# Adaptive-norm transformer layer on one core: the projection stage laid out in even slots, and the residual rows formed in the output stage

## The chip, the cores and the metric

One core of one Trainium2 chip runs the whole kernel as one program. The metric is the device time of one execution in microseconds (us). The engines are TensorE (PE in the profile, PEld for its weight loads), VectorE (DVE), ScalarE (ACT), GpSimd (POOL) and SyncE (SP), which issues the DMAs here.

## What is computed

The reference is one layer over x of shape 16 x 1024 x 256 (batches, rows, features), cut here to what the change touches:

```
sa, ca, ga, ... = six vectors of 256 per batch, from silu(c) @ wmod
h  = layernorm(x) * (1 + ca) + sa
xn = layernorm(h) * ln_gamma + ln_beta
q, k, v = xn @ Wq + bq, xn @ Wk + bk, xn @ Wv + bv      # 16 heads of 16
q, k = rope(q), rope(k)
out = softmax(mask(q k^T / 4)) v                         # causal, 1024 x 1024 per head
x  = x + ga * (h + out @ Wo + bo)
# then layernorm(x) * (1 + cb) + sb and a routed feed-forward part over the first two batches' rows
```

All is float32 to the output. The term `x + ga * h` of each row is called its residual row below. Written with the first norm `n = layernorm(x)`, it is `x + n * (ga * (1 + ca)) + ga * sa`; the factor `ga * (1 + ca)` is the row `M_A2` of the table of modulation rows (`mods_d`), and the constant part is in the output bias.

## The kernel before

The program has five stages, one after the other, each in a block of its own: `phase0` (tables and modulation rows), `phase1` (norms, projections, rope), `phase2` (attention), `phase3` (output projection and residual) and `phase4` (feed-forward). The change is in `phase1` and `phase3`. A batch is T = 8 tiles of 128 rows by 256 features.

**The projection stage** (`phase1`) treats 16 batches. For one batch:

- `take_x` (L443) and `join_x` on VectorE make mean and variance of x; `root` on ScalarE (L558) and `invert_x` on VectorE (L455, L457) turn them into a scale `rsx` and an offset `nmx` per row.
- `first_norm` (L566, ScalarE) writes n into `h1`; `scale_h` (L652, GpSimd) multiplies by 1 + ca into `h`; `shift_h` (L463, VectorE) adds sa; `take_h` (L471) and `join_h` (L477) make the statistics of h; `invert_h` (L483, L485) and `second_norm` (L574, ScalarE) normalise it.
- `residual` (L659, L662, GpSimd) turns `h1` into the residual rows in two passes, and SyncE stores them to `resid_d` in DRAM (L403).
- `turn_x` (L690, TensorE) transposes a tile, `copy_x` (L582, ScalarE) brings it to SBUF as `x_t`.
- `project` (L701, TensorE) makes 2 x 512 columns of q or k at a time: 4 products per batch, n = 0 to 63 in all. `values` (L708, L710) makes v tile by tile, `copy_v` (L591, ScalarE) takes it.
- Of product n, `multiply` (L497, four passes over PSUM) and `combine` (L506, L507) on VectorE do the rope. Then it is split into three bfloat16 parts: `high` (L599, ScalarE), `take_rest` (L512, VectorE), `middle` (L603, ScalarE), `low` (L666, GpSimd). SyncE stores the parts (L417) and v (L409).

The order on each engine is written by hand: a loop `steps` runs over batches b and half steps j = 0 to 7 and calls `both(nx, fr, b, j)` on every engine. In half step j batch b is projected, batch fr = b + 1 is normed, and of batch nx = b + 2 the statistics are taken. On VectorE this is

```
if j % 2 == 0:
    multiply(n)              # the product that TensorE makes in this same half step
else:
    if n: take_rest(n - 1)
    combine(n)
```

with shifts in j = 1 to 4, `join_h` in j = 5 and `invert_h` in j = 6; `second_norm` follows in j = 6 and 7, and TensorE turns the next batch's first tiles there. `xin`, `h1`, `h` and `mods` have two buffers each.

**The output stage** (`phase3`) goes over the 16 batches with two buffers, 8 tiles each. Per batch SyncE loads attention output `att` (2 MB), the residual rows `res` (1 MB), the gate row and the bias (`load`, L1157 to L1160), always after it has stored the batch before (`store`, L1166). VectorE makes `wg` = Wo times gate (L1188), then per tile reciprocals (L1196), `norm` (L1200), and at last adds the residual row to the product (L1206). ScalarE's only work is `copy` of the turned tile `n_t` (L1217). TensorE per tile: 4 transposes (L1231), 2 transposes (L1239), and the product with the bias (L1249, L1251). GpSimd does nothing.

## Time and profile before

| | us |
|---|---|
| median of 3 runs (lowest, highest) | 3242.84 (3241.46, 3244.81) |
| the profiled execution | 3240.84 |
| its span in the profile | 3239.1 |

| stretch of the profiled execution, from the span's start | us |
|---|---|
| projection stage | 60 to 738 |
| attention stage | 738 to 2622 |
| output stage | 2622 to 2894 |
| feed-forward stage | 2894 to 3239 |

Busy time of an engine counts its computing instructions, not issues of DMAs and not waits. An engine's instruction is recorded from its start to its end, and neighbours overlap a little, so what an instruction costs its engine in a run is read from one start to the next (called its pitch below). An instruction that is held back after it was started shows a longer duration.

### The profile page before, as it was taken

Reading aid. Unit: us, or ns where it says so; the run is one execution under the profiler, and the core shown is the slowest. Engines: PE = TensorE matmul, PEld = TensorE weight load, DVE = VectorE, ACT = ScalarE, POOL = GpSimd, SP = SyncE. Lnnn points to the kernel's source line nnn. Section 1 sums busy time; section 2 is a strip of 40 time slices with the busy share of each in tenths; the row PEclk is TensorE's granted clock in tenths of the full one; section 3 lists DMA queues with packets and bytes.
Section 4 is the critical chain, followed back from the end, with each engine's and each line's share of the span. In section 5 each row is a group of like instructions: output and inputs, shape, how many; then the busy total and the mean of one; then the engine's idle time right before and its main releaser. Section 6 shows DMA issues by size and latency. Waiting matters only on the chain. (4 is left out here: it accounts for less than half of the span.)

```text
span 3239.1 us, 48169 instructions
## 1 busy us (share of the span) xinstructions
PE 2817.5 (87%) x17587; PEld 1353.4 (42%) x17587; DVE 2278.7 (70%) x3286; ACT 1765.1 (54%) x3595; POOL 948.2 (29%) x1174
## 2 busy tenths in 40 slices
PE   1677777775999999999999999999999879975997
PEld 0333333331444444444444444444444347753664
DVE  4899999986777777777777777777777435553231
ACT  1455555550777777777777777777777721111111
POOL 2677777762112221121222211212222100003231
PEclk7888888885999999999999999999999989987999
DMA  2355555547344444445444444444444146663332
GB/s 77 127 192 192 192 192 192 191 156 169 71 97 96 92 93 91 99 100 100 97 94 92 94 91 100 100 100 97 91 94 93 42 188 258 258 230 102 79 103 54
DMA packets 173951, 402.96 MB, mean 124 GB/s; under 512 B 33147, under 2 KB 85792, under 8 KB 157107
## 3 DMA queue, kind: packets, MB, share of 16 engines
q1 hardware_dynamic: 167572, 391.36, 46.0%
q0 software_dynamic: 6144, 8.52, 1.5%
q8 instruction: 142, 2.33, 0.3%
q14 instruction: 93, 0.75, 0.1%
HBM read 240.65 MB, written 161.31 MB: 124 GB/s over the span
## 5 line engine op out<-in xcount | busy, mean ns | idle before, releaser
L962 DVE TENSOR_REDUCE mx<-ps 128x2 f32<-128x1024 f32 (+3 forms) x1216 | 1371.4, 1167 | 396.8 <-PE ps L1050 301.6
L1008 ACT ACTIVATE prob<-ps 128x512 f32<-128x512 f32 (+1 forms) x2560 | 1252.0, 560 | 538.4 <-PE ps L1068 529.7
L1043 PE MATMUL ps<-k_rows,q_rows 96*128 96x512 bf16 (+3 forms) x3072 | 911.2, 332 | 38.1 <-DMA k_rows<-k_parts 31.4
L1068 PE MATMUL ps<-q_rows,k_rows 99*128 99x512 bf16 (+3 forms) x3072 | 907.2, 328 | 14.7 <-ACT prob L1008 6.1
L901 POOL TENSOR_SCALAR_AFFINE_SELECT prob<-prob 128x512 f32<-128x512 f32 x512 | 320.0, 637 | 1451.3 <-ACT prob L1008 1451.3
L1087 PE MATMUL ps<-prob,v_rows 128*32 128x512 f32 (+3 forms) x6144 | 628.2, 496 | 0.0
L1068 PEld LDWEIGHTS ps<-q_rows,k_rows 99*128 99x128 bf16 x3072 | 273.1, 98 | 599.0 <-ACT prob L1008 360.2
L1043 PEld LDWEIGHTS ps<-k_rows,q_rows 96*128 96x128 bf16 x3072 | 290.2, 98 | 268.5 <-DVE mx L962 60.7
L1050 PE MATMUL ps<-mask_b,unit_b 128*128 128x128 bf16 (+2 forms) x1408 | 348.6, 248 | 0.0
L701 PE MATMUL ps<-x_t,w_all 128*128 128x512 f32 x512 | 233.2, 598 | 23.2 <-ACT x_t L582 23.2
L1087 PEld LDWEIGHTS ps<-prob,v_rows 128*32 128x32 f32 x6144 | 134.3, 108 | 245.8 <-ACT prob L1008 122.9
L690 PE MATMUL ps<-ident,h 128*128 128x128 f32 x256 | 48.2, 319 | 206.5 <-ACT h L574 203.9
L1217 ACT COPY n_t<-ps 128x256 f32<-128x256 f32 x128 | 47.7, 373 | 231.8 <-PE ps L1239 231.8
L666 POOL TENSOR_TENSOR stage<-rest,stage 128x1024 bf16<-128x1024 f32 x64 | 147.8, 2309 | 75.5 <-ACT stage L603 75.5
L710 PE MATMUL ps<-w_all,x_t 128*128 128x256 f32 x512 | 167.5, 456 | 0.0
L1485 DVE SCALAR_TENSOR_TENSOR y<-ps,gx,gate 128x256 f32<-128x256 f32 x32 | 15.5, 484 | 195.4 <-PE ps L1576 195.4
L1050 PEld LDWEIGHTS ps<-mask_b,unit_b 128*128 128x128 bf16 x1408 | 139.5, 99 | 22.9
L652 POOL TENSOR_TENSOR h<-h,mods_b 128x256 f32<-128x256 f32 x128 | 111.2, 890 | 121.2 <-ACT h L566 121.1
L701 PEld LDWEIGHTS ps<-x_t,w_all 128*128 128x128 f32 x512 | 95.2, 191 | 121.5 <-issue 92.7
L1251 PE MATMUL ps<-wg,n_t 128*128 128x256 f32 x512 | 145.7, 407 | 0.0
L497 DVE SCALAR_TENSOR_TENSOR m<-ps,bcol,cos_t 128x512 f32<-128x512 f32 x128 | 89.6, 740 | 61.1 <-PE ps L701 61.1
L690 PEld LDWEIGHTS ps<-ident,h 128*128 128x128 f32 x256 | 33.6, 158 | 234.7 <-ACT h L574 223.0
(154 smaller groups left out, 2745.3 us busy)
## 6 DMA issues: line engine op xcount, KB each, us to landing
k_rows<-k_parts SPq DMA_DIRECT2D x384, 128.0 KB, 7.4
v_ones<-v_st SPq DMA_DIRECT2D x64, 512.0 KB, 9.2
v_rows<-v_ones SPq DMA_DIRECT2D x64, 512.0 KB, 9.3
att<-o_sb SPq DMA_DIRECT2D x128, 256.0 KB, 3.2
att_b<-att SPq DMA_DIRECT2D x16, 2048.0 KB, 9.8
q_parts<-stage SPq DMA_DIRECT2D x128, 192.0 KB, 3.6
k_parts<-stage SPq DMA_DIRECT2D x128, 192.0 KB, 3.2
q_rows<-q_parts SPq DMA_DIRECT2D x64, 384.0 KB, 4.5
```

What stands on the lines that cost most here:

```text
L652: pool.tensor_tensor(h[:, p, t, :], h1[:, p, t, :], mods[:, p, M_CA1, :], ALU.mult).then_inc(h_mul, 1)
L666: pool.tensor_tensor(parts(n, 2), rest[:, n % 2], parts(n, 1), ALU.subtract).then_inc(lo_done, 1)
L701: ins = pe.matmul(ps[:, PS_QK + c, :], w_all[:, k, c * P:(c + 1) * P], x_t[:, blk, k, :], start=(k == 0), stop=(k == KC - 1))
L710: ins = pe.matmul(o, x_t[:, t // 4, k, t % 4 * P:t % 4 * P + P], w_all[:, k, 2 * D:3 * D], start=False, stop=(k == KC - 1))
L901: pool.affine_select(out=own, in_=own, compare_op=ALU.is_ge, fill=0.0, base=0, pattern=[[0, HG], [1, P]], channel_multiplier=-1).then_inc( ...
L962: dve.tensor_reduce(dst, src, AX.X, ALU.max).then_inc(a_free, 1)
L1008: nc.scalar.activation(prob[:, (g * NPC + i) % RING, h, 0:w], src, ACT.Exp).then_inc(exp_done, 1)
L1043: ins = pe.matmul(ps[:, at, col:col + w], q[0:ROWS, g, h, i * P:(i + 1) * P], k[0:ROWS, g, h, k0:k0 + w], start=(r == 0), stop=True, skip_ ...
L1050: ins = pe.matmul(own, unit_b[:, :], mask_b[:, :].rearrange("p (o n) -> p o n", o=1) .to_broadcast([P, per, P]), start=False, stop=True, s ...
L1068: ins = pe.matmul(ps[:, PS_B + bank(g, n), at:at + w], k[0:AUG, g, h, j * P:(j + 1) * P], q[0:AUG, g, h, q0:q0 + w], start=True, stop=True)
L1087: ins = pe.matmul(ps[32 * h:32 * h + 32, PS_O, col:col + w], v[:, g, j, h, :], prob[:, (g * NPC + i) % RING, h, at:at + w], start=(j == 0) ...
L1251: ins = pe.matmul(o, n_t[:, r % 2, k, :], wg[:, p, k, :], start=False, stop=(k == KC - 1))
```

## The change

Projection stage: the loop over slots s = -23 to 133 takes the place of `steps`. Product n is made by TensorE in slot 2n; VectorE multiplies it in slot 2n+1 and combines it in slot 2n+2; ScalarE's `high` is in slot 2n+3, `take_rest` in slot 2n+4, `middle` in slot 2n+5, `low` in slot 2n+6. The norms are spread over the slots one tile at a time, `batch_at(s, lead)` giving the batch and tile whose turn it is: `take_x` has lead 23, `first_norm` 17, `modulate` (GpSimd, was `scale_h`) 16, `take_h` 15 with the shift inside it, `second_norm` 5 (`normed_in`), `turn_x` one slot later and `copy_x` two. `h1` is gone: `first_norm` writes over `xin`, which has three buffers. `residual` and its store are gone from this stage; `rsx` and `nmx` are kept for all batches.

Output stage: it loads x itself (`xb`) and the row `M_A2` (`a2`) in place of `resid_d`, after the small rows and `att`. ScalarE makes n again (`first_norm`, two tiles ahead, before the copy of each tile), GpSimd makes the residual rows in two passes, VectorE waits for them (`r_done`) before its addition.

```
-            def both(nx, fr, bk, j):
-                n = bk * NP + j // 2
...
+            def slot(s):
+                n = (s - 1) // 2
+                if s % 2 == 1 and 0 <= n < B * NP:
+                    multiply(n)
+                n = (s - 2) // 2
+                if s % 2 == 0 and 0 <= n - 1 < B * NP:
+                    take_rest(n - 1)
+                if s % 2 == 0 and 0 <= n < B * NP:
                     combine(n)
...
+                b, k = batch_at(s, 15)
+                if b is not None:
+                    take_h(b, k)
+                    if k == T - 1:
+                        join_h(b)
+                b, k = batch_at(s, 23)
+                if b is not None and k < 4:
+                    take_x(b, k)
...
@@ ScalarE @@
+            def slot(s):
+                b, k = batch_at(s, 19)
+                if b is not None and k == 0:
+                    root(b, 0, agx, agx_done, sdx_done)
+                b, k = batch_at(s, 7)
+                if b is not None and k == 0:
+                    root(b, 1, agh, agh_done, sdh_done)
+                for tiles, b in turned_in(s - 1):
+                    for t in tiles:
+                        copy_x(b, t)
+                n = (s - 3) // 2
+                if s % 2 == 1 and 0 <= n < B * NP:
+                    high(n)
...
+                n = (s - 5) // 2
+                if s % 2 == 1 and 0 <= n < B * NP:
+                    middle(n)
+                b, k = batch_at(s, 17)
+                if b is not None:
+                    first_norm(b, k)
...
@@ GpSimd @@
-            def residual(b, tiles):
...
+            def slot(s):
+                b, k = batch_at(s, 16)
+                if b is not None:
+                    modulate(b, k)
+                n = (s - 6) // 2
+                if s % 2 == 0 and 0 <= n < B * NP:
+                    low(n)
...
@@ phase3 @@
         def load(sp, b, p):
-            sp.dma_start(att[:, p], att_d[b].rearrange("g p t -> p g t")).then_inc(att_in[p], DMA)
-            sp.dma_start(res[:, p], resid_d[b]).then_inc(res_in[p], DMA)
             sp.dma_start(gate[:, p], mods_d[b, M_GA, :].partition_broadcast(P)).then_inc(small_in[p], DMA)
             sp.dma_start(ob[:, p], out_bias_d[b]).then_inc(small_in[p], DMA)
+            sp.dma_start(att[:, p], att_d[b].rearrange("g p t -> p g t")).then_inc(att_in[p], DMA)
+            reuse(sp, r_done, b * T - T)
+            sp.dma_start(xb[:, p], x[b].rearrange("(t p) d -> p t d", p=P)).then_inc(x_in[p], DMA)
+            sp.dma_start(a2[:, p], mods_d[b, M_A2, :].partition_broadcast(P)).then_inc(x_in[p], DMA)
...
+            def first_norm(b, t):
+                p = b % 2
+                if t == 0:
+                    act.wait_ge(x_in[p], (b // 2 + 1) * 2 * DMA)
+                    reuse(act, x2_done, b * T - T)
+                nc.scalar.activation(res[:, p, t, :], xb[:, p, t, :], ACT.Identity, bias=nmx[:, b, t:t + 1],
+                                     scale=rsx[:, b, t:t + 1]).then_inc(r_norm, 1)
+
             def work(b, half, p):
                 for t in range(T):
+                    n = b * T + t + 2
+                    if n < B * T:
+                        first_norm(n // T, n % T)
                     act.wait_ge(nt_done, b * T + t + 1)
...
+        @block.gpsimd
+        def _(pool):
+            def residual(b, t):
...
+                pool.tensor_tensor(res[:, p, t, :], res[:, p, t, :], a2[:, p, :], ALU.mult).then_inc(r_mul, 1)
+                pool.wait_ge(r_mul, b * T + t + 1)
+                pool.tensor_tensor(res[:, p, t, :], res[:, p, t, :], xb[:, p, t, :], ALU.add).then_inc(r_done, 1)
```

The order on VectorE in the projection stage, before, is that of half steps 0 to 3 of a middle batch (m, qr and rest belong to rope and split, h and sth to the next batch's norm):

```order
L497 SCALAR_TENSOR_TENSOR m<-ps,bcol,cos_t 128x512 x2
L497 SCALAR_TENSOR_TENSOR m<-ps,bcol,sin_t 128x512 x2
L463 TENSOR_TENSOR h<-h,mods_b 128x256 x2
L512 TENSOR_TENSOR rest<-qr,stage 128x1024
L506 TENSOR_TENSOR qr<-m 128x512
L507 TENSOR_TENSOR qr<-m 128x512
L471 BN_STATS sth<-h 128x6 x2
L463 TENSOR_TENSOR h<-h,mods_b 128x256 x2
```

The same place after the change, from the combine of a slot with s mod 8 = 2 to the combine two slots later:

```order
L475 RECIPROCAL rsh<-sd 128x8
L477 SCALAR_TENSOR_TENSOR nmh<-agh,rsh 128x8
L461 TENSOR_TENSOR h<-h,mods_b 128x256
L464 BN_STATS sth<-h 128x6
L441 BN_STATS stx<-xin 128x6 x2
L489 SCALAR_TENSOR_TENSOR m<-ps,bcol,cos_t 128x512 x2
L489 SCALAR_TENSOR_TENSOR m<-ps,bcol,sin_t 128x512 x2
L461 TENSOR_TENSOR h<-h,mods_b 128x256
L464 BN_STATS sth<-h 128x6
L441 BN_STATS stx<-xin 128x6 x2
L504 TENSOR_TENSOR rest<-qr,stage 128x1024
L498 TENSOR_TENSOR qr<-m 128x512
L499 TENSOR_TENSOR qr<-m 128x512
```

The shift of a tile and its statistics now follow each other, once in every slot.

SyncE's queue in the output stage, before, for one batch:

```order
L1166 DMA sum_rows<-x 128x8x256
L1157 DMA att_b<-att 128x4x1024
L1158 DMA res_b<-resid 128x2048
L1159 DMA gate_b<-mods 128x256
L1160 DMA ob_b<-out_bias_parts 3x256
```

and after:

```order
L1124 DMA sum_rows<-x 128x8x256
L1113 DMA gate_b<-mods 128x256
L1114 DMA ob_b<-out_bias_parts 3x256
L1115 DMA att_b<-att 128x4x1024
L1117 DMA x_b<-in_L_attn_x 128x8x256
L1118 DMA a_b<-mods 128x256
```

One transfer more, the small rows moved ahead of `att`, and x in rows of 1 KB where the residual rows came in pieces of 8 KB.

## Rows read from the trace of the kernel before

**Rows 1.** Stretch's start:end, its length, busy us (instructions) of PE, PEld, DVE, ACT, POOL
```profile
60.00:738.00 678.00, 454.69 (x1408) 240.69 (x1408) 596.32 (x1152) 341.04 (x673) 480.89 (x449) 0.82 0.55 180
2622.00:2894.00 272.00, 253.72 (x1408) 191.41 (x1408) 149.57 (x416) 47.72 (x128) 0.00 (x0) 0.98 0.65 243
```
**Rows 2.** Groups of instructions by shape, 100 to 700 us (busy us, mean ns)
```profile
L463 DVE TENSOR_TENSOR h<-h,mods_b 128x256 f32<-128x256 f32 x118 | 111.0, 979 | 0.0
L599 ACT CAST stage<-qr 128x1024 bf16<-128x1024 f32 x59 | 61.2, 1038 | 2.4 <-DVE qr L507 2.4
L566 ACT ACTIVATE h<-xin,nmx,rsx 128x256 f32<-128x256 f32 x118 | 64.7, 599 | 0.0
```
**Rows 3.** Durations of single lines (min/median/max ns), whole run
```profile
L463 DVE TENSOR_TENSOR h<-h,mods_b x128: 402/937/2350, 74.1 to 685.7; 128x256 f32<-128x256 f32 x128
L471 DVE BATCH_NORM_STATS2 sth<-h x128: 401/407/417, 80.7 to 689.6; 128x6 f32<-128x256 f32 x128
L659 POOL TENSOR_TENSOR h<-h,mods_b x128: 713/732/1712, 77.9 to 698.9; 128x256 f32<-128x256 f32 x128
```
**Rows 4.** Timeline of VectorE over one batch (start us, us)
```profile
420.60 1.41 DVE L497 SCALAR_TENSOR_TENSOR m<-ps,bcol,cos_t 128x512 f32<-128x512 f32 x2 [3.00 <-PE ps L701]
...
434.58 0.76 DVE L463 TENSOR_TENSOR h<-h,mods_b 128x256 f32<-128x256 f32 x2
435.27 1.21 DVE L512 TENSOR_TENSOR rest<-qr,stage 128x1024 f32<-128x1024 f32 x1
436.40 0.68 DVE L506 TENSOR_TENSOR qr<-m 128x512 f32<-128x512 f32 x1
...
438.27 2.64 DVE L463 TENSOR_TENSOR h<-h,mods_b 128x256 f32<-128x256 f32 x2
440.83 1.40 DVE L497 SCALAR_TENSOR_TENSOR m<-ps,bcol,cos_t 128x512 f32<-128x512 f32 x2
...
444.24 0.64 DVE L477 BATCH_NORM_AGGREGATE agh<-sth 128x2 f32<-128x6 f32 x8
...
461.56 1.41 DVE L497 SCALAR_TENSOR_TENSOR m<-ps,bcol,cos_t 128x512 f32<-128x512 f32 x2 [3.00 <-PE ps L701]
```
**Rows 5.** Timeline of GpSimd beside it
```profile
437.64 2.13 POOL L666 TENSOR_TENSOR stage<-rest,stage 128x1024 bf16<-128x1024 f32 x1 [2.91 <-ACT stage L603]
439.72 1.77 POOL L659 TENSOR_TENSOR h<-h,mods_b 128x256 f32<-128x256 f32 x2
```
**Rows 6.** Timeline of TensorE in the same batch
```profile
423.82 3.60 PE L701 MATMUL ps<-x_t,w_all 128*128 128x512 f32 x8
...
429.80 3.60 PE L701 MATMUL ps<-x_t,w_all 128*128 128x512 f32 x8
...
450.42 1.18 PE L690 MATMUL ps<-ident,h 128*128 128x128 f32 x4 [11.05 <-ACT h L574]
```
**Rows 7.** Timeline of VectorE: the first product taken, the last combine
```profile
95.91 0.75 DVE L497 SCALAR_TENSOR_TENSOR m<-ps,bcol,cos_t 128x512 f32<-128x512 f32 x1 [10.45 <-PE ps L701]
...
730.50 0.69 DVE L507 TENSOR_TENSOR qr<-m 128x512 f32<-128x512 f32 x1
```
**Rows 8.** Timelines in one batch of the output stage
```profile
2728.30 0.39 SPq L1166 DMA_DIRECT2D out<-x  x1
2740.38 0.37 ACT L1217 COPY n_t<-ps 128x256 f32<-128x256 f32 x1 [1.55 <-PE ps L1239]
2741.76 0.28 PE L1249 MATMUL ps<-ob_b,ones 3*128 3x256 bf16 x1
2744.86 0.39 SPq L1166 DMA_DIRECT2D out<-x  x1
```
**Rows 9.** The residual rows' load there (L1158), 16 issues: us to landing
```profile
DMA to landing us min/median/max: 9.9/11.8/17.2
```
**Rows 10.** The DMAs' rate from 2728 to 2745 us, in 40 slices
```profile
GB/s 0 0 27 381 386 388 378 248 214 198 246 369 443 434 376 376 434 424 434 405 405 405 472 492 337 501 424 347 376 240 24 19 0 0 0 0 0 0 0 0
```
**Rows 11.** The same from 89 to 100 us (from slice 20 on x's load)
```profile
GB/s 0 0 0 0 0 477 477 477 179 298 477 387 179 238 268 149 220 168 279 398 376 398 376 398 372 384 361 358 376 395 346 190 116 0 0 0 0 0 0 0
```

More of the change, by code:

```diff
@@ L358, in phase1 @@
         v_st = sb("v_st", [P, 2, NG, T, NV], F32)
-        x_in, mod_in = pair("p1_x_in"), pair("p1_mod_in")
+        x_in = tuple(sem(f"p1_x_in{r}") for r in range(RING))
+        mod_in = tuple(sem(f"p1_mod_in{r}") for r in range(RING))
         stx_done, sth_done = sem("p1_stx"), sem("p1_sth")
@@ L381, in parts, with batch_at, normed_in, turned_in @@
             return stage[:, b % 2, part, 2 * which:2 * which + 2, blk * W:(blk + 1) * W]
-        def steps(both):
-            for b in range(B):
-                fr = b + 1 if b + 1 < B else None
-                nx = b + 2 if b + 2 < B else None
-                for j in range(2 * NP):
-                    both(nx, fr, b, j)
+        START = -23
+        END = B * T + 6
+        def batch_at(s, lead):
+            b, k = (s + lead) // T, (s + lead) % T
+            return (b, k) if 0 <= b < B else (None, None)
+        def normed_in(s):
+            b, k = batch_at(s, 5)
+            if b is not None and k < 7:
+                yield ((0, 1), (2, 3), (), (4,), (5,), (6,), (7,))[k], b
+        def turned_in(s):
+            return normed_in(s - 1)
         @block.sync
@@ L534, in both @@
-                if nx is not None and j == 7:
-                    join_x(nx)
-            dve.memset(eps[:, :], EPS)
-            for b in range(2):
-                for k in range(2):
-                    take_x(b, range(4 * k, 4 * k + 4))
-                join_x(b)
-                if b == 0:
-                    invert_x(0)
-            for k in range(4):
-                shift_h(0, (2 * k, 2 * k + 1))
-            for k in range(4):
-                take_h(0, (2 * k, 2 * k + 1))
-            join_h(0)
@@ L553, in _ @@
+                b, k = batch_at(s, 23)
+                if b is not None and k < 4:
+                    take_x(b, k)
+                    if k == 3:
+                        join_x(b)
+            dve.memset(eps[:, :], EPS)
+            for s in range(START, END):
+                slot(s)
         @block.scalar
@@ L630, in _ @@
-            act.wait_ge(ones_set, 1)
-            root(0, 0, agx, agx_done, sdx_done)
-            first_norm(0, range(T))
-            root(1, 0, agx, agx_done, sdx_done)
-            root(0, 1, agh, agh_done, sdh_done)
-            second_norm(0, range(T))
-            for t in range(4):
-                copy_x(0, t)
-            steps(both)
-            high(B * NP - 1)
-            middle(B * NP - 1)
+            def slot(s):
+                b, k = batch_at(s, 19)
+                if b is not None and k == 0:
+                    root(b, 0, agx, agx_done, sdx_done)
+                b, k = batch_at(s, 7)
+                if b is not None and k == 0:
+                    root(b, 1, agh, agh_done, sdh_done)
[5 more added lines that the diff above has]
+                    high(n)
+                if s % 2 == 0 and 2 <= s <= B * T:
+                    for t in (s - 2, s - 1):
+                        copy_v(t // T, t % T)
+                n = (s - 5) // 2
[4 more added lines that the diff above has]
+                    first_norm(b, k)
+                for tiles, b in normed_in(s):
+                    for t in tiles:
+                        second_norm(b, t)
@@ L642, in _ @@
+            act.wait_ge(ones_set, 1)
+            for s in range(START, END):
+                slot(s)
         @block.gpsimd
         def _(pool):
-            def scale_h(b, tiles):
-                p = b % 2
-                if 0 in tiles:
-                    pool.wait_ge(mod_in[p], (b // 2 + 1) * DMA)
-                    reuse(pool, xt_done, b * T - T)
-                for t in tiles:
-                    pool.wait_ge(h1_done, b * T + t + 1)
-                    pool.tensor_tensor(h[:, p, t, :], h1[:, p, t, :], mods[:, p, M_CA1, :], ALU.mult).then_inc(h_mul, 1)
@@ L666, in low @@
                 pool.tensor_tensor(parts(n, 2), rest[:, n % 2], parts(n, 1), ALU.subtract).then_inc(lo_done, 1)
[L668 to L682 removed]
+            def slot(s):
[5 more added lines that the diff above has]
+                    low(n)
+            pool.memset(v_st[:, :, :, :, :], 1.0).then_inc(ones_set, 1)
+            for s in range(START, END + 1):
+                slot(s)
         @block.tensor
@@ L1189, in work @@
                 ins.then_inc(wg_done, 1)
-                dve.wait_ge(res_in[p], half * DMA + DMA)
                 for t in range(T + 2):
```

230 lines of the change are left out of this document (84 added, 146 removed).

## Prediction

> **What bounds the kernel now.** I read the busy times by stretch first, then groups and single lines, then timelines of one batch in both changed stages. Attention and feed-forward are untouched, so only two stretches count. In the projection stage VectorE is busy 596 of 678 us, TensorE 455, GpSimd 481 [rows 1]: VectorE bounds it. But that busy time is not all work. The shift h<-h,mods_b takes 402 ns at best and 979 in the mean, while the statistics of an equal tile never leave 401 to 417 [rows 2, 3]. The row that swells has two inputs in SBUF, the one that doesn't has one. Rows 4 and 5 show why: two shifts need 0.76 us at 434.58 and 2.64 at 438.27, where GpSimd was in `low` from 437.64 to 439.77. So a two-input row of VectorE (shift, rest, the two combines) and a row of GpSimd exclude each other, and a held row goes on about 0.13 us before GpSimd's recorded end: GpSimd holds 2.0 us per `low` and 0.6 per 256-column row. Two such streams alternate: GpSimd's two L659 take 1.77 there, 0.89 each instead of 0.7 [rows 5].
>
> The output stage is TensorE's, 254 busy of 272 us [rows 1], with a period of 2744.86 - 2728.30 = 16.56 us per batch [rows 8].
>
> **Projection stage: VectorE's own work.** Pitches, from start to start or the duration less the 0.08 of overlap [rows 3, 4]: multiply 4 x 0.66 = 2.64, rest 1.13, combine 2 x 0.60, shift 0.345, a tile's statistics 0.33, eight aggregates 0.56, and an estimated 0.2 for each of four short rows. A batch before: 4 x (2.64 + 1.13 + 1.21) + 8 x 0.345 + 16 x 0.33 + 2 x 0.56 + 0.8 = 29.9. Its period is 461.56 - 420.60 = 40.96 [rows 4]. 3.0 of it is the wait for the next batch's first product [rows 4], so 8.1 are holds by GpSimd and small waits, of the 24 x 0.6 + 4 x 2.0 = 22.4 that GpSimd holds per batch.
>
> After the change: the wait of 3.0 goes, since product n is made a slot before it is multiplied, and TensorE, with 5.98 us for a product and two value tiles [rows 6] plus two transposes, 6.6 in all, is done a slot ahead. Shift and statistics of one tile now follow each other and the second waits for the first: 0.41 + 0.04 in place of 0.345, 0.8 per batch; aggregates likewise, 0.2. Own work 30.9. GpSimd loses both residual passes and keeps 8 x 0.6 + 4 x 2.0 = 12.8 of holding. What it still costs must be walked through, since its place is fixed by a chain: `high` waits for the combine of the slot before.
>
> Let C be the end of the combine in a slot with s mod 8 = 2 (the piece shown above). ScalarE [rows 2]: `high` C+0.1 to 1.15, `middle` to 2.1, a first norm to 2.6. GpSimd: modulate C+2.7 to 3.4, `low` holds C+3.4 to 5.4. VectorE: inverts 0.4, shift and statistics 1.18, statistics of x 1.84, multiply 4.48; its shift meets `low`, gets through at 5.4 and ends at 5.8; statistics and x to 6.8; rest, combine: **9.2**. Held 0.9. The other three pairs of slots, same way: from slot 4, `join_x` and the root ahead of `high` push ScalarE back by 2.4, rest is through before GpSimd, but the first combine waits for modulate and the second for all of `low`: **10.3**. From slot 6, multiply ends at 4.1 and the shift waits to 5.4: **8.6**. From slot 0, with `join_h` and the other root, rest waits for `low` (5.5 to 7.4) and a combine for modulate: **10.3**. Sum 38.4 per batch, 7.5 of it held. Bounds: nothing held gives 30.9, everything held 43.7. The nearest row is the kernel before, where 8.1 of 22.4 held, 36%: by that share 4.6 and a period of 35.5. I take the walk, because the chain puts `low` where the two-input rows come; both ends stay for the range.
>
> **Sum of the stage.** Before, from the first product row to the last combine: 731.2 - 95.9 = 635.3 [rows 7]. After: the norms of batch 0 run tile by tile through three engines, the first product row comes an estimated 2 us earlier. Batches 0 to 12 have full slots: 13 x 38.4 = 499. Batch 13 has no statistics of x: walked, 36. Batches 14 and 15 have no front work left, VectorE needs 5.0 and TensorE 6.6 per pair of slots: 2 x 26.5 = 53. That is 588, less 1.4, as C lies that far before the first product row of its next slot, 587. The last parts come out 2 later behind the last combine, since `rest` and `middle` run later. Stage: -48 - 2 + 2, about **-49**. Each us of the full batch's period is worth 13.
>
> Costed at nothing: the store of the residual rows gone (x is loaded 17 us before its use), x's third buffer. If loads were late, VectorE would stand at `take_x`.
>
> **Output stage.** (a) ScalarE gets 128 first norms of 0.6 [rows 2] beside copies of 0.37, within a per-tile pace of 1.93: covered. (b) GpSimd gets 256 rows of 0.73, 1.5 per tile, covered. (c) What is not covered is the landing of x. ScalarE's queue has the next batch's first norm ahead of the copy of tile 6, so that copy now waits for x and a2 of the next batch, and those are issued only after this batch's first instruction on SyncE, the store. In the trace the residual rows were issued about 1.05 after the store and landed after 11.8 [rows 9], 12.85; the DMAs run at over 400 GB/s nearly to that point [rows 10], so bytes ahead of x push it back: gate row +0.35, a2 +0.35, and x in 1 KB rows runs at 360 to 400 GB/s [rows 11] against 405 to 470 for the last part here, +0.3. Landing at 13.85. Then 0.55 to the copy, 0.37 for it, 0.06: TensorE's product of tile 6 can start at 14.8 after the store, where it starts at 2741.76 - 2728.30 = 13.46 [rows 8]. **+1.4 per batch.** (d) The late x makes GpSimd late: its rows for three tiles run from 0.8 to 5.3 after the landing, and VectorE's two `wg` rows, two inputs in SBUF, come at 4.1. The first waits 0.4, the second a whole row: **+1.1**, and TensorE waits for VectorE there. Together 2.5, for the 14 batches 1 to 14 that load in stride: +35, and +1 for edges: **+36**. Bounds: landing 1.4 earlier and nothing is lost, 0; a landing as late as 17.2 [rows 9] was the first, behind two batches' loads, and is not taken, but 1 us later gives +50.
>
> The Trainium skill bears on (c): DMA: Bandwidth & Descriptors, Specifications, says that from 512 B on a transfer runs at line rate. By it x would cost no more in 1 KB rows than in 8 KB pieces, and the sum would be 4 us lower. The rates of this trace differ [rows 10, 11], and the measured one is used.
>
> **Sum:** 3240.8 (the profiled execution; its span is 3239.1) - 49 + 36 = 3228, I give **3227**. The median of the runs shown is 2.0 above that execution.
>
> **Rivals.**
> 1. x lands in time (the DMAs finish earlier than first in, first out suggests). For it: the last slices of [rows 10] are nearly empty, a straggler decides. Against: the same straggler stays. 3227 - 36 = 3191.
> 2. GpSimd's holds keep their old share, 35.5 per batch: 13 x 2.9 = 38 less, 3189. For it: a walk with fixed durations locks more than engines do. Against: before, half of GpSimd's rows were residual rows beside multiply, which cost nothing.
> 3. Slower: `low` meets more than I walked. Its place is the second combine and the rest; if it also takes the first combine in the pairs from slots 2 and 6, 1 to 1.5 us each, the period is 41 and the time 3227 + 34 = 3261. It decides from 38.4 + 14/13 = 39.5 on, 40 for 0.2%. For it: the bound of 43.7. Against: in those pairs `low` ends at 5.4, before rest.
> 4. TensorE's clock. In the trace it stood at half its full rate after the gap of 11.05 us at 450 [rows 6], mean 0.82 over the stage [rows 1]; the change has shorter gaps, 2 to 4 us in every pair of slots. If the half rate stayed all through, TensorE would need 53 per batch and bound it: 13 x 14.6 + 53 more, 3470. Against: TensorE works 6.6 of 8.6 to 10.3 us in every pair.
> 5. Nothing moves: the product was never late but once per batch, and holds eat its 3.0: 3241.
>
> On rival 4 the Trainium skill speaks against the change: TensorE: Matmul & The Clock Gate, HAM oscillation, tells of kernels where waits between short groups of matmuls throw the clock back every time. No row here has such short gaps at the lower rate, so it gets a small chance.
>
> **How the numbers follow.** Forecast 0.44, rival 1 0.12, rival 2 0.19, rival 3 0.20, rival 4 0.02, rival 5 0.03. About 0.2% (6.5 us) is what a measurement of this kernel can tell from no change. Faster: both faster rivals and 0.34 of the forecast's 0.44 (its own range is 3211 to 3243), 0.65. Same: 0.08 of it, rival 5 and a little of rival 3, 0.13. Slower 0.22. The range 3190 to 3253 takes in either faster rival alone and rival 3 up to 40.4 per batch; both faster ones together (3153) and rival 4 are left out.
>
> **What would show it.** Right: no wait of VectorE for TensorE's product in batches 1 to 13; a period of 38.4; its shifts and combines, not its statistics, above their best durations; clock 1.0 through the stage; the stage's end near 689 us. In the output stage a period near 19, ScalarE idle at L1176 until DMA x_b, and `wg` rows of 0.8 to 1.1. Wrong: a period of 16.6 there, or VectorE's two-input rows near their best, or VectorE idle at `rest` or `take_x`.

## The result, and the profile after

| | before | after |
|---|---|---|
| median of 9 runs, us (lowest, highest) | 3243.09 (3241.09, 3244.90) | 3254.40 (3250.15, 3264.99) |
| span of the profiled execution | 3239.1 | 3254.3 |
| attention stage's first product, from the span's start | 760.0 | 715.1 |
| output stage: mean from one store to the next (14 stores of `out<-x`) | 16.57 | 20.72 |

The change makes the kernel slower: ratio 1.0042, 95% interval 1.0030 to 1.0054. The forecast was 3227, faster, with a range from 3190 to 3253, and the median lies just outside it. The two stages went opposite ways, as forecast, with other sizes: the attention stage starts 44.9 us earlier, and the output stage takes 59 us more.

**By stretch.** These are the projection and the output stage of the changed kernel, columns as in [rows 1]:

```profile
60.00:693.00 633.00, 484.04 (x1408) 252.75 (x1408) 604.26 (x1152) 332.07 (x673) 277.65 (x193) 0.85 0.53 163
2577.00:2908.00 331.00, 275.42 (x1408) 205.29 (x1408) 153.36 (x414) 107.99 (x256) 183.39 (x256) 0.91 0.62 208
```

The same instructions (x1408, x1152) stand in 633 us where there were 678, and VectorE is now busy in 604 of them: it waits for almost nothing. In the output stage TensorE's busy time rose from 254 to 275 for the same 1408 products while its granted clock fell from 0.98 to 0.91 [rows 1], and 56 us of the stage are now idle on it, where there were 18.

**Projection stage, VectorE.** One batch of the timeline, cut to combines and shifts (pairs of slots end with the L499 rows at 402.77, 412.68, 430.81 and 441.41, and with one at 422.42 that isn't shown):

```profile
402.77 0.68 DVE L499 TENSOR_TENSOR qr<-m 128x512 f32<-128x512 f32 x1
403.38 0.41 DVE L461 TENSOR_TENSOR h<-h,mods_b 128x256 f32<-128x256 f32 x1
...
410.14 2.61 DVE L498 TENSOR_TENSOR qr<-m 128x512 f32<-128x512 f32 x1
412.68 1.21 DVE L499 TENSOR_TENSOR qr<-m 128x512 f32<-128x512 f32 x1
...
418.19 1.47 DVE L461 TENSOR_TENSOR h<-h,mods_b 128x256 f32<-128x256 f32 x1
...
430.81 2.61 DVE L499 TENSOR_TENSOR qr<-m 128x512 f32<-128x512 f32 x1
...
437.37 1.85 DVE L461 TENSOR_TENSOR h<-h,mods_b 128x256 f32<-128x256 f32 x1
...
441.41 0.68 DVE L499 TENSOR_TENSOR qr<-m 128x512 f32<-128x512 f32 x1
```

and GpSimd beside it:

```profile
409.10 3.10 POOL L626 TENSOR_TENSOR stage<-rest,stage 128x1024 bf16<-128x1024 f32 x1
417.25 2.13 POOL L626 TENSOR_TENSOR stage<-rest,stage 128x1024 bf16<-128x1024 f32 x1
430.31 2.57 POOL L626 TENSOR_TENSOR stage<-rest,stage 128x1024 bf16<-128x1024 f32 x1
436.81 2.13 POOL L626 TENSOR_TENSOR stage<-rest,stage 128x1024 bf16<-128x1024 f32 x1
```

Two of the four `low` (409.10, 430.31) meet a combine, which then takes 2.61 in place of 0.68; the other two (417.25, 436.81) meet a shift, 1.47 and 1.85 in place of 0.41. The combine that began the batch at 402.77 comes again at 441.41: 38.6 here, and 38.48 in the mean over the full batches, where 38.4 was forecast.

**Output stage.** Timelines of one batch. SyncE's queue, with the store as zero of the batch:

```profile
2703.09 0.38 SPq L1124 DMA_DIRECT2D out<-x  x1
2703.51 0.58 SPq L1113 DMA_DIRECT2D gate_b<-mods  x1
...
2705.31 0.54 SPq L1115 DMA_DIRECT2D att_b<-att  x1
2705.89 0.58 SPq L1117 DMA_DIRECT2D x_b<-in_L_attn_x  x1
...
2723.86 0.38 SPq L1124 DMA_DIRECT2D out<-x  x1
```

ScalarE, which has the next batch's first norm ahead of the copy of tile 6 (the a_b row comes in last of the two loads that it waits for):

```profile
2718.79 0.60 ACT L1176 ACTIVATE res_b<-x_b,nmx,rsx 128x256 f32<-128x256 f32 x1 [4.97 <-DMA a_b<-mods]
2719.30 0.35 ACT L1186 COPY n_t<-ps 128x256 f32<-128x256 f32 x1
```

and TensorE:

```profile
2716.45 0.38 PE L1225 MATMUL ps<-ident,norm 128*128 128x128 f32 x2
2719.70 0.28 PE L1235 MATMUL ps<-ob_b,ones 3*128 3x256 bf16 x1 [2.88 <-ACT n_t L1186]
2719.91 1.13 PE L1237 MATMUL ps<-wg,n_t 128*128 128x256 f32 x4
...
2721.30 2.08 PE L1237 MATMUL ps<-wg,n_t 128*128 128x256 f32 x4
```

The product of tile 6 starts 16.61 after the store, where it started 13.46 after it [rows 8]: 3.15 later. From there to the next store it is 4.16, where it was 3.10 [rows 8]: the second group of four products takes 2.08 instead of 1.13, at the lower of TensorE's two clocks, 1.2 GHz (granted clock 0.65 in the mean from 2719.7 to 2723.8), after a wait of 2.88. Together 4.2 per batch, 14 of them 59.

The 14 batches with a load behind them aren't alike: they take 18.2 to 22.6 us. In the mean the product of tile 6 starts 16.55 after the store, 3.1 later than before, and 4.19 pass from there to the next store, 1.1 more than before. In ten of them products at the batch's end come at the half clock, and these take 19.7 to 22.6; the four without it take 18.2 to 19.1.

**The DMAs in that wait**, 17 us from the store on, in 40 slices of 0.425 us:

```profile
GB/s 0 0 205 393 388 386 378 349 354 133 117 19 60 58 106 345 395 434 405 434 414 443 405 424 424 381 414 354 376 357 349 347 347 284 164 48 0 0 0 0
```

Slices 10 to 15 (2.6 us) move 82 GB/s in the mean. Before, the same place had four slices of 198 to 248 [rows 10]. The bytes are the same but for the additional a2 row; what stands at this place now is the gate row, behind the store. SyncE's issue of `att` comes later too, 2.22 after the store where it was 0.42 in the kernel before.

### The profile page after: what moved, and what is told of

It is laid out like the page before. It is cut to its first block and busy times, and to the rows that moved or that the text cites. A ratio compares the mean times of both kernels' runs of the same rounds, so it can differ in the third digit from the quotient of the medians.

```text
span 3254.3 us, 48508 instructions
## 1 busy us (share of the span) xinstructions
PE 2869.1 (88%) x17587; PEld 1379.0 (42%) x17587; DVE 2287.8 (70%) x3286; ACT 1816.2 (56%) x3723; POOL 927.7 (29%) x1174
## 5 line engine op out<-in xcount | busy, mean ns | idle before, releaser
L995 PE MATMUL ps<-k_rows,q_rows 96*128 96x512 bf16 (+3 forms) x3072 | 911.0, 332 | 42.8 <-DMA k_rows<-k_parts 36.1
L657 PE MATMUL ps<-x_t,w_all 128*128 128x512 f32 x512 | 262.6, 661 | 0.0
L622 POOL TENSOR_TENSOR h<-xin,mods_b 128x256 f32<-128x256 f32 x128 | 129.1, 1012 | 311.1 <-ACT xin L546 311.1
L1164 DVE TENSOR_TENSOR x<-ps,res_b 128x256 f32<-128x256 f32 x128 | 54.4, 425 | 161.4 <-PE ps L1237 161.4
L1237 PE MATMUL ps<-wg,n_t 128*128 128x256 f32 x512 | 159.8, 439 | 0.0
L657 PEld LDWEIGHTS ps<-x_t,w_all 128*128 128x128 f32 x512 | 109.3, 222 | 114.4 <-issue 111.8
L1200 POOL TENSOR_TENSOR res_b<-res_b,a_b 128x256 f32<-128x256 f32 x128 | 93.1, 727 | 142.2 <-ACT res_b L1176 142.2
```

What stands on the lines that cost most here:

```text
L622: pool.tensor_tensor(h[:, p, t, :], xin[:, r, t, :], mods[:, r, M_CA1, :], ALU.mult).then_inc(h_mul, 1)
L657: ins = pe.matmul(ps[:, PS_QK + c, :], w_all[:, k, c * P:(c + 1) * P], x_t[:, blk, k, :], start=(k == 0), stop=(k == KC - 1))
L995: ins = pe.matmul(ps[:, at, col:col + w], q[0:ROWS, g, h, i * P:(i + 1) * P], k[0:ROWS, g, h, k0:k0 + w], start=(r == 0), stop=True, skip_ ...
L1237: ins = pe.matmul(o, n_t[:, r % 2, k, :], wg[:, p, k, :], start=False, stop=(k == KC - 1))
```

## The experiments

Four theories stood for the output stage. **Order**: the small rows ahead of `att` cost the DMAs time out of all proportion to their bytes, and x lands late. **Place**: what costs is that the copy of tile 6 stands behind the norm that waits for x. **Clock**: the half clock after the wait is what costs. **Holds**: GpSimd's rows holding VectorE's `wg` rows. For the projection stage the forecast's chain (each `low` comes where a two-input row of VectorE comes) stood against a plain share of GpSimd's time, and against a gain that came from the residual rows' going alone. Every kernel is the changed one with the edit shown; before ran beside them at 3242.69, 3242.17 and 3242.74 in the three sets.

### small_last: the small rows behind the loads

```
-            sp.dma_start(gate[:, p], ...)
-            sp.dma_start(ob[:, p], ...)
             sp.dma_start(att[:, p], ...)
             reuse(sp, r_done, b * T - T)
             sp.dma_start(xb[:, p], ...)
             sp.dma_start(a2[:, p], ...)
+            sp.dma_start(gate[:, p], ...)
+            sp.dma_start(ob[:, p], ...)
```

> The changed kernel, with the gate row and the bias loaded last in the output stage (att, x, a2, gate, bias) instead of first. Landing theory: in the changed kernel's trace the DMA engines are nearly idle for about 2 us while the small rows pass between the store and att, so x lands 15.5 us after the store and not 13.9. With the small rows last, x should land near 13.7, the period of the output stage should fall from 20.9 to 18 to 19, and the time from 3254 to about 3218. Lock theory (the loss in the output stage is GpSimd's new rows holding up VectorE): nothing changes, 3254.

3227.02, ratio to before 0.9953 (0.9937 to 0.9970): 27 us below the changed kernel. From one of its stores on, the rate in the same 40 slices, and ScalarE's norm of that batch (its store is at 2695.83):

```profile
GB/s 0 0 287 388 388 386 313 135 205 219 292 434 405 414 376 424 395 434 443 414 405 424 362 388 373 354 345 349 352 342 347 98 0 0 0 0 0 0 0 0
```
```profile
2709.48 0.60 ACT L1176 ACTIVATE res_b<-x_b,nmx,rsx 128x256 f32<-128x256 f32 x1 [2.59 <-DMA a_b<-mods]
```

The hole is gone but for four slices of 135 to 292, as before the change. In this batch x and a2 are there 13.65 after the store, where it was 15.70 in the batch shown of the changed kernel; but 13.65 is the earliest of this kernel's 14 batches. In the mean it is 14.27 against 15.63: 1.36 us for 128 KB and 1.5 KB, where the forecast had 0.35. From one store to the next it is 18.56 instead of 20.72, and only 1.36 of that difference is the landing itself: the half clock is now at the end of one batch in place of ten, and from the product of tile 6 to the next store it is 3.25 in the mean instead of 4.19. The time is 9 us above what this run was expected to give by the landing theory, and 27 below what it expected if GpSimd's holds were the loss.

### gate_first and bias_first: one small row at a time

```
gate_first: gate, att, x, a2, ob
bias_first: ob, att, x, a2, gate
```

> The changed kernel, with only the gate row (128 pieces of 1 KB from one row of DRAM) ahead of att in the output stage, and the bias (3 pieces of 512 bytes) last. If the gate row makes the DMA engines stand nearly idle behind the store, the time stays near 3254. If the bias does, it is near 3227, what both rows last gave.

> The mirror image: only the bias ahead of att, the gate row last. Near 3227 if the gate row makes the idle stretch, near 3254 if the bias does; both between the two if each has a share.

gate_first 3260.48 (1.0048, 1.0031 to 1.0065), bias_first 3235.28 (0.9974, 0.9964 to 0.9983). The rates from a store on, gate_first and then bias_first:

```profile
GB/s 0 0 289 388 388 388 361 352 188 125 164 84 142 80 108 316 357 443 414 405 424 434 424 386 443 400 410 347 369 354 347 352 345 252 188 63 0 0 0 0
```
```profile
GB/s 0 0 279 393 386 390 386 376 161 293 241 376 357 279 308 270 395 405 405 414 395 443 342 405 386 371 373 357 347 349 296 164 96 39 24 24 2 0 0 0
```

The gate row alone makes the hole (seven slices of 80 to 188) and costs all that both rows together cost, and 6 us more. The bias row makes hardly one, but strings out the end of the loads in this batch, and costs 8 us against small_last. Since batches differ, here are the means of 14: when ScalarE's norm that waits for x and a2 starts, behind the store, when SyncE issues `att` in the batch shown, and the time from store to store.

| kernel | norm starts (lowest, highest) | `att` issued | store to store |
|---|---|---|---|
| small_last | 14.27 (13.65, 15.05) | 0.43 | 18.56 |
| bias_first | 14.96 (13.94, 16.02) | 0.93 | 19.44 |
| changed kernel | 15.63 (14.23, 16.48) | 2.22 | 20.72 |
| gate_first | 15.88 (14.90, 16.99) | 1.05 | 21.03 |

```profile
2696.26 0.58 SPq L1113 DMA_DIRECT2D att_b<-att  x1
```
```profile
2706.13 1.20 SPq L1114 DMA_DIRECT2D att_b<-att  x1
```

These are the issues of small_last (store at 2695.83) and gate_first (store at 2705.08). A rival of the row's own cost is SyncE's time: two more issues stand ahead of `att` in the changed kernel, and `att` is issued 1.8 later than in small_last. That alone isn't it. In gate_first `att` is issued 1.17 earlier than in the changed kernel and x is there no earlier; and gate_first and bias_first issue `att` at nearly the same time, yet with the gate row x comes 0.9 later. Between bias_first and small_last, 0.7, the issue may be what counts. So order is shown, and the row that costs most is named: 128 pieces of 1 KB that all read one row of DRAM. Why they leave the engines idle, these runs don't tell: a DMA engine that does nothing shows no reason.

### x_first: x and a2 ahead of `att`

```
             sp.dma_start(gate[:, p], ...)
             sp.dma_start(ob[:, p], ...)
+            reuse(sp, r_done, b * T - T)
+            sp.dma_start(xb[:, p], ...)
+            sp.dma_start(a2[:, p], ...)
             sp.dma_start(att[:, p], ...)
```

> The changed kernel, with x and a2 loaded before att in the output stage. Landing theory: ScalarE's norm of the next batch never waits, the period is 16.6 to 17.0 and the time 3254 - 59 = 3195 (up to 3202 if att, now last, is needed a little before it lands). Lock theory: GpSimd's rows are all still there, so at least 1 us per batch stays and the time is above 3210.

3200.48 (0.9873, 0.9857 to 0.9890), the mean from store to store 16.68: but for 0.1 the pace of before, with the gate row still first. Issue to landing of x, and the norm's wait in one batch:

```profile
DMA to landing us min/median/max: 5.6/6.8/12.7
```
```profile
2711.73 0.60 ACT L1176 ACTIVATE res_b<-x_b,nmx,rsx 128x256 f32<-128x256 f32 x1 [0.32 <-DMA a_b<-mods]
```

So all but 0.1 per batch of the output stage's loss hangs on when x lands. `att` is 2 MB, x 1 MB; `att` can take the later place. The norm waits for x in five of the 14 batches, by 1.4 at most, and TensorE never waits for the copy behind it.

### norm_after_copy: the same loads, another place for the norm

```
-                    n = b * T + t + 2
-                    if n < B * T:
-                        first_norm(n // T, n % T)
                     act.wait_ge(nt_done, b * T + t + 1)
...
                     nc.scalar.copy(n_t[:, t % 2], ...)
+                    n = b * T + t + 1
+                    if n < B * T:
+                        first_norm(n // T, n % T)
```

> The changed kernel, with ScalarE's first norm one tile ahead and behind the copy of the tile, not two ahead and before it; all transfers as in the changed kernel. Landing theory: x lands as late as before, but no copy stands behind it, so the period is 16.6 plus what GpSimd's rows, now right at the batch's start, hold up VectorE's two gate rows: 0 to 1.2 us. Time 3195 to 3212. If the DMAs' volume itself were the loss, the time would stay at 3254.

3203.92 (0.9880, 0.9863 to 0.9896), store to store 17.31. x lands when it did in the changed kernel, but nothing that TensorE needs stands behind it. Landing of x, and VectorE's `wg` rows:

```profile
DMA to landing us min/median/max: 11.0/11.6/13.5
```
```profile
2704.05 1.76 DVE L1146 TENSOR_TENSOR wg<-wo,gate_b 128x256 f32<-128x256 f32 x2
```

Place is shown too: the late transfer and the wait ahead of the copy are both needed for the loss. The two `wg` rows, behind the batch's last addition, take 1.76 together where they take 0.75 unheld: a hold by GpSimd, as in the forecast's step (d). The pace is 0.7 us above that of before: 0.4 in 11 of the 13 batches, and the rest from two of 19.3 and 18.9, in which products at the half clock follow a wait for VectorE.

### filler: TensorE kept at work in the wait

```
+                        if t == T:
+                            for _ in range(3):
+                                pe.matmul(ps[:, 6, :], ident[:, :], mask[:, :], start=True, stop=True)
                         pe.wait_ge(nt_copied, b * T + r + 1)
```

Nobody reads these products.

> The changed kernel, with three products of 512 columns per batch that nobody reads (the identity by the mask into a free PSUM bank), issued by TensorE just ahead of the product that waits for the late copy. They fill 2.6 us of a wait of 2.9. Clock theory: a part of the loss is that TensorE's granted clock falls to the half in that wait and the next 2 to 4 us of work run at it. Then the clock stays at 1.0, and the time falls by 1 to 1.5 us in each of 14 batches, to about 3237, although TensorE has 40 us more to do. If the clock costs nothing, the time is the same or up to 5 us more.

3251.81 (1.0031, 1.0018 to 1.0044), 2.6 us below the changed kernel, whose interval overlaps this one. The clock theory had given 3237. In the profile, by windows of both kernels over the same stretch, the changed one first (the stretch, then busy us as in [rows 1], then the granted clock):

```profile
2600.00:2860.00 260.00, 215.31 (x1105) 160.25 (x1103) 121.12 (x330) 84.30 (x201) 142.88 (x200) 0.91 0.64 216
```
```profile
2600.00:2860.00 260.00, 239.06 (x1237) 168.71 (x1235) 130.23 (x341) 87.48 (x208) 149.31 (x208) 1.00 0.67 224
```

The clock is at its full 2.4 GHz, and yet store to store is only 0.8 shorter (19.96). The timelines of the filler kernel, TensorE and VectorE, tell a part of why:

```profile
2717.79 0.28 PE L1238 MATMUL ps<-ob_b,ones 3*128 3x256 bf16 x1 [1.04 <-ACT n_t L1186]
...
2723.09 0.44 PE L1225 MATMUL ps<-ident,norm 128*128 128x128 f32 x2 [1.82 <-DVE norm L1157]
```
```profile
2720.78 1.62 DVE L1146 TENSOR_TENSOR wg<-wo,gate_b 128x256 f32<-128x256 f32 x2
```

The end of the batch is as short as before: from the product of tile 6 to the next store it is 3.10 in every batch, where the changed kernel has 4.19 in the mean. So the half clock costs 1.09 per batch, 15 us in all. The fast end also brings the `wg` rows into GpSimd's residual rows: 1.62 instead of 0.95, and TensorE waits 1.82 for VectorE behind them. That hold by itself would cost nothing, since TensorE has still to wait for x in the same batch; in the changed kernel the batch whose store is at 2638.16 has the same wait of 1.82 and a further one of 2.86 for the copy. But here the three products, 2.7 us with the last one's end, fill more than what is left of the wait. In the next batch they end at 2737.81, 0.7 behind the copy that TensorE could have used at 2737.10; in the mean of 14 batches the product of tile 6 starts 0.46 after its copy, where it was 0.06. The fillers take back 0.4 of what they bring, so the 0.8 is what this edit is worth and not the price of the clock.

### old_order: before's projection stage without its residual rows

The projection stage of before, `residual` and its store taken out; the output stage of the changed kernel.

> Only one half of the change: the projection stage keeps the half steps of the kernel before, but its residual passes and their store are gone, and the output stage is the changed one. If moving the residual rows out is what shortened the projection stage, GpSimd holds 12.8 us per batch in place of 22.4, a third of the difference is VectorE's gain, 3.5 us of 40.96 per batch, and the attention stage starts about 50 us earlier than in the kernel before, as it does in the changed kernel (45). If the slots did it, VectorE still waits 3 us per batch for the next batch's first product, and the residual rows lay mostly beside multiplies: the period falls by at most 1.5 and the stage ends at most 20 us earlier. The output stage loses its 59 either way, so the time is 3250 by the first and 3275 or more by the second.

3297.79 (1.0183, 1.0161 to 1.0206). The attention stage starts at 759.5, before at 760.0: taking 9.6 us of GpSimd's rows out of each batch gains nothing by itself. VectorE's waits from 120 to 640 us, before the change and in old_order:

```profile
DVE m L497 <- PE ps L701: 39.0, 13, 3.2
DVE rsx L455 <- ACT sd L558: 5.7, 13, 0.6
```
```profile
DVE m L486 <- PE ps L677: 49.5, 13, 4.9
DVE rsx L444 <- ACT sd L547: 23.7, 13, 1.8
```

and the group of the first combine from 120 to 620 us, before the change and in old_order:

```profile
L506 DVE TENSOR_TENSOR qr<-m 128x512 f32<-128x512 f32 x49 | 53.0, 1081 | 0.0
```
```profile
L495 DVE TENSOR_TENSOR qr<-m 128x512 f32<-128x512 f32 x49 | 39.7, 810 | 0.0
```

The combines got shorter (53.0 to 39.7 us over the window), and VectorE waits instead: 49.5 for the product and 23.7 for the root, where the kernel before waited 39.0 and 5.7. So without the new order of the slots none of the stage's -44.9 is there. Whether the new order would give all of it with the residual rows left in the stage isn't shown: that kernel wasn't run. The output stage's loss stands alone in this run: 3297.79 - 3242.17 = 55.6 us.

### roots_later and low_first: the chain that places `low`

roots_later, ScalarE's slot: `root` in slots 19 and 7 ahead of a batch no longer stands in front of `high` and `middle`.

```
-                b, k = batch_at(s, 19)
-                if b is not None and k == 0:
-                    root(b, 0, agx, agx_done, sdx_done)
-                b, k = batch_at(s, 7)
...
                 if s % 2 == 1 and 0 <= n < B * NP:
                     middle(n)
+                b, k = batch_at(s, 19)
...
```

low_first, GpSimd's slot:

```
-                b, k = batch_at(s, 16)
-                if b is not None:
-                    modulate(b, k)
                 n = (s - 6) // 2
                 if s % 2 == 0 and 0 <= n < B * NP:
                     low(n)
+                b, k = batch_at(s, 16)
...
```

> The changed kernel, with ScalarE's two square roots of a batch issued behind high and middle of their slot, no longer ahead of them. By the walk of the prediction the pairs from slots 0 and 4 are 10.3 because the root makes high wait for VectorE's aggregates; without that they should be 9.4 and 8.9, the full batch's period 36.1 in place of 38.6, the time 32 us less than the changed kernel's: 3222. If GpSimd's holds were spread evenly and not by the chain of waits, nothing would change.

> The changed kernel, with GpSimd's low ahead of modulate in the even slots. By the walk low then holds from C+2.2 to 4.2, beside multiply, and only modulate meets the shift: pairs 9.2, 8.6, 10.0 and 7.4, a period of 35.2 in place of 38.6, the time 41 us less: 3213. If what counts is how long GpSimd holds in all (12.8 us, unchanged), the time is the same, 3254.

roots_later 3226.14 (0.9946, 0.9930 to 0.9963), attention from 685.3; low_first 3233.81 (0.9977, 0.9967 to 0.9987), from 691.8. One batch apart on VectorE, roots_later and then low_first:

```profile
306.13 1.39 DVE L489 SCALAR_TENSOR_TENSOR m<-ps,bcol,cos_t 128x512 f32<-128x512 f32 x2
...
342.51 1.39 DVE L489 SCALAR_TENSOR_TENSOR m<-ps,bcol,cos_t 128x512 f32<-128x512 f32 x2
```
```profile
301.72 1.38 DVE L489 SCALAR_TENSOR_TENSOR m<-ps,bcol,cos_t 128x512 f32<-128x512 f32 x2
...
338.54 1.38 DVE L489 SCALAR_TENSOR_TENSOR m<-ps,bcol,cos_t 128x512 f32<-128x512 f32 x2
```

36.4 and 36.8 in place of 38.5, with not one instruction of VectorE or GpSimd less. A share of GpSimd's time can't tell these kernels apart; the walk can: it gave 36.1 for the first (0.3 too low) and 35.2 for the second (1.6 too low, and the time 21 us above the 3213 expected). What meets the holds changes places, by groups from 150 to 600 us, roots_later and low_first:

```profile
L461 DVE TENSOR_TENSOR h<-h,mods_b 128x256 f32<-128x256 f32 x100 | 109.3, 1093 | 0.0
L498 DVE TENSOR_TENSOR qr<-m 128x512 f32<-128x512 f32 x49 | 33.9, 692 | 0.0
```
```profile
L504 DVE TENSOR_TENSOR rest<-qr,stage 128x1024 f32<-128x1024 f32 x50 | 91.1, 1822 | 0.0
```

With the roots later `low` falls on the shift, and the combine is near its best; with `low` first it falls on `rest`, which takes 1822 where 1.2 us are its own.

### both_orders: a version that beats both kernels

roots_later and low_first together, and the loads in the order x, a2, att, gate, ob. This order of loads wasn't run by itself.

> Both orders together, and in the output stage x and a2 first, then att, then the small rows. By the walk the pairs are 8.0, 8.6, 8.0 and 7.4, a period of 32, near VectorE's own work of 30.9; the projection stage ends another 84 us earlier and the output stage has a period of 16.6 without a wait for att: 3254 - 84 - 60 = 3110. If TensorE's clock, at the half in parts of every period, becomes the bound, the period stops at 34 to 35 and the time at 3140.

**3118.79 (3117.34 to 3120.33), ratio to before 0.9617, 0.9601 to 0.9633.** The projection stage's stretch, columns as in [rows 1], and VectorE's groups from 150 to 600 us:

```profile
60.00:615.00 555.00, 447.63 (x1408) 234.88 (x1408) 528.32 (x1152) 332.24 (x673) 257.31 (x193) 0.91 0.60 185
```
```profile
L461 DVE TENSOR_TENSOR h<-h,mods_b 128x256 f32<-128x256 f32 x100 | 57.2, 572 | 0.0
L504 DVE TENSOR_TENSOR rest<-qr,stage 128x1024 f32<-128x1024 f32 x57 | 80.4, 1411 | 0.0
```

The time is 9 us above the 3110 of the walk and 21 below what a bound by TensorE's clock would have given. A batch takes 32.7, where the walk had 32 (304.29 to 337.01, from one first multiply to the next), 1.8 above the forecast's 30.9 for VectorE's own work: `low` now starts with the multiplies (GpSimd at 304.72, VectorE at 304.29), whose product comes from PSUM, and only its last part meets the shift behind them (0.90 at 306.92). In the output stage the stores are 16.57 apart, as before the change. The two edits of order give 5.8 per batch together, where alone they gave 2.1 and 1.7.

## Why the prediction was wrong

**Its sign was wrong, by step (c) of the output stage: x was to land 13.85 us after the store, and the norm that waits for it starts at 15.63 in the mean.** Point by point:

- *Wait for the next batch's first product gone, 3.0 per batch*: right. Between 120 and 640 us the profile after has no wait of VectorE for TensorE.
- *Walk of the holds, 38.4 per batch as 9.2, 10.3, 8.6, 10.3*: right. 38.48, and the pairs 9.21, 10.32, 8.68, 10.43 in the trace. In the last of them the place is another than walked: `rest` is through before `low`, and the first combine waits for it (2.61 at 410.14). Rival 2 (holds keep their share, 35.5) is refuted, as are rival 3 (`low` meets more, 41) and, for this stage, rival 5 (nothing moves).
- *Batches 0 to 12 full, batch 13 36, batches 14 and 15 26.5*: from first multiply to first multiply batch 0 took 34.4, 4 less than a full one, batches 1 to 12 took 38.5, batch 13 34.6 and batch 14 26.5.
- *First product 2 us earlier*: wrong. The first product row comes 5 later (95.91 before, [rows 7]), as this line of VectorE shows:

```profile
101.01 1.41 DVE L489 SCALAR_TENSOR_TENSOR m<-ps,bcol,cos_t 128x512 f32<-128x512 f32 x2 [4.40 <-PE ps L657]
```

  The slots put the norms of later batches among those of batch 0, ahead of this product: ScalarE's root at 91.51 has waited 2.49 for VectorE's aggregates, the copy of `x_t` stands behind it, and TensorE waited 3.93 for that copy. The forecast left this out; it is 7 us. From the first product row to the last combine's end it is 583.5 us (101.01 to 684.48) where the forecast had 587, by batches 0 and 13, and from that end to the attention stage's first product it is 30.6 where it was 28.8, the 2 forecast. So the stage is -51.8 + 5.1 + 1.8 = -44.9. The forecast's own terms, -48 - 2 + 2, are -48; its -49 is a slip of 1.
- *Output stage (c), landing at 13.85 after the store, +1.4 per batch*: **the step that failed.** It took over the issue and the landing of the old residual rows, 12.85, and added bytes at the engines' full rate, "gate row +0.35" among them. Moved directly behind the store, the two small rows cost 1.36 in the mean: 15.63 with them ahead of `att`, 14.27 with them last. The other 0.8 of the error is there in small_last too, 14.27 where the rest of the sum had given 13.5; which of a2, x's rate and its place makes it isn't shown. TensorE's product of tile 6 so starts 16.55 after the store and not at 14.8: 3.1 later than before in place of 1.4, and 14 x 1.7 = 24 us of the forecast's error. Rival 1 (x in time) fell with it. That small_last, which puts the rows last, came out at the forecast's 3227 is luck: the projection stage gained less than forecast there and the output stage lost less.
- *(d) GpSimd's rows hold `wg`, +1.1*: right in size, by luck. A hold there comes just behind the store, and TensorE then still has to wait for x, so (c) and (d) overlap and don't add up; the forecast added them. Where the copy is early (norm_after_copy) there is no such wait, and the hold costs 0.4 in most batches. What makes the changed kernel's batch 1.09 longer is the half clock at its end.
- *Rival 4, the clock*: asked in the wrong stage. In the projection stage the granted clock is 0.85 in the mean, 0.82 before, and costs nothing while VectorE bounds it. In the output stage, where TensorE bounds, every landing made TensorE wait, from 1.5 to 3.8 us, and ten of 14 batches had a slow end. The forecast looked only at whether x was late, not at what such a wait does to the products behind it. The Trainium skill, TensorE: Matmul & The Clock Gate, HAM oscillation, describes waits for a transfer that throw the clock back each time; the trace agrees in ten batches of 14, with 0.65 granted behind the wait of 2.88. The half clock costs 1.09 per batch, by the filler run's 3.10 against 4.19.
- *x in 1 KB rows slower, +0.3*: the rates support it. In the changed kernel's slices above `att`, in pieces of 4 KB, runs at 381 to 443 GB/s and x behind it at 347 to 376. By the Trainium skill, DMA: Bandwidth & Descriptors, Specifications, both would be at line rate; the measurement speaks against it here, by some 15%. No run changes the size of the pieces alone, so that it is the size isn't shown. The forecast's "405 to 470" for the old residual rows is a smoothed reading: their slices in [rows 10] go from 337 to 501.

The sum by what was measured: 3240.8 - 44.9 + 59 + 1 (later stages) = 3256, the profiled span and the 1.7 around it.

What stays open: why the gate row leaves the engines idle. Its address, its 128 reads of one DRAM row, its following a store, or what SyncE's queue does with it weren't tried apart; x_first shows that with x behind it instead of `att` the hole is shallower (116 to 294 GB/s), no more.

## What to carry to other kernels

A transfer's price is its place in the queue as well as its bytes: put what an in-order engine waits for first, broadcast rows last, and put no wait for the next batch's load ahead of work that the bounding engine needs. Where two engines exclude each other, walk the chain that fixes when the holder runs: cutting its work can gain nothing, and reordering two lines can gain 2 us per batch. When a walk ends in a forecast close to zero, the terms priced by bytes are the ones to bound again, by the nearest row that shows the same transfer at the same place. Two delays of one batch add up only if nothing waits between them: what TensorE loses ahead of a wait for a landing is free. And a run is read by the mean of its batches, since the two batches shown differ by 2.05 in x's landing (15.70 and 13.65) and the means by 1.36.

## What was not expected of the hardware

- **A row broadcast to 128 partitions behind a store.** With 128 KB of it next in the queue the DMAs moved 19 to 133 GB/s for 2.6 us; with the bias row it cost 1.36 us of landing in the mean, four times the 0.35 that the forecast had for its bytes; alone ahead of the loads (gate_first) it had the norm start 15.88 after the store. This profile line is of x_first, from a store on, where x follows the small rows:

```profile
GB/s 0 0 291 390 390 390 363 339 260 116 238 211 130 221 255 294 270 320 347 337 342 385 318 419 407 404 414 443 404 404 424 404 270 193 116 29 0 0 0 0
```

- **The half clock behind a wait of 2.9 us.** In the batch shown, a TensorE that had been busy 12.6 of the 13 us from 2703 to 2716, at a granted clock of 0.92 and then 1.00, ran the products behind a wait of 2.88 first at 2.4 GHz (1.13 for four) and then at 1.2 GHz (2.08 for four).
- **A delay ahead of a wait is free until the wait is filled.** TensorE waited 1.8 us for the held `wg` rows in batches of both kernels. In the changed kernel that shortened the wait for x and cost nothing; with the fillers in that wait it made the product of tile 6 late.
- **What holding costs goes by its place.** The same 12.8 us of GpSimd's reads per batch cost VectorE 7.6 us in the changed kernel, 5.5 with the roots later, 1.8 with both orders (each period less the forecast's 30.9). The Trainium skill, SBUF — State Buffer, Who interferes with whom, gives the rule: a VectorE instruction with two SBUF inputs contends with a GpSimd instruction that reads SBUF, one with at most one SBUF input doesn't. The rows agree: 0.41 us free and 1.85 held for one shift, and in both_orders a multiply at its usual 1.39 for two (304.29) beside a `low` (304.72).
